# A graph attention layer on one core: the first stage in another order, and the first loads cut in halves

## What is computed

```python
h = jnp.maximum(_layernorm(x, axis=-1), 0.0)
# inside the layer, with node_features = h
h = node_features @ W.T + b_W
a1, a2 = (a_vec[:D_OUT], a_vec[D_OUT:])
e = (h @ a1)[:, None] + (h @ a2)[None, :] + b_a[0]
e = jnp.where(e > 0, e, 0.2 * e)
scores = jnp.where(adjacency_matrix > 0, e, jnp.float32(NEG_INF))
attention = jax.nn.softmax(scores, axis=1)
h_prime = attention @ h
# and outside it
x = x + h_prime
```

## Time and profile before

| | us |
|---|---|
| median of 3 runs | 201.71 (201.53 to 201.79) |
| profiled execution, its own time | 202.36 |
| span of the profiled execution | 200.8 |
| TensorE busy | 194.9 (97%) |
| VectorE busy | 183.0 (91%) |
| ScalarE busy | 147.9 (74%) |
| GpSimd busy | 52.4 (26%) |
| transfers | 75.66 MB, 377 GB/s over the span |

### The profile page before, as it was taken

One profiled execution on the slowest core, in us unless ns is written; L12 is line 12 of the kernel. 1 busy time (PEld: TensorE's weight loads), 2 busy tenths in 40 slices (PEclk: granted clock), 3 DMA queues, 4 the chain that ended last, 5 costly groups with the idle time before them and its releaser, 6 DMA issues.

```text
span 200.8 us, 7230 instructions
## 1 busy us (share of the span) xinstructions
PE 194.9 (97%) x3183; PEld 189.2 (94%) x3183; DVE 183.0 (91%) x265; ACT 147.9 (74%) x192; POOL 52.4 (26%) x66
## 2 busy tenths in 40 slices
PE   7969999999999999999999999999999999999993
PEld 7648889999999999999999999999999999999993
DVE  4779999999998799897999999999999999999745
ACT  2679879898882777689988888899588888996000
POOL 1002479699995010205000000072000000510000
PEclk9999999999999999999999999999999999999999
DMA  5999999999999999999999999999999999997012
GB/s 181 376 417 418 407 403 423 421 418 415 422 432 408 418 423 419 416 421 418 415 419 423 419 418 421 421 411 421 419 418 418 415 421 416 418 383 226 6 43 66
DMA packets 15968, 75.66 MB, mean 377 GB/s; under 512 B 1600, under 2 KB 5952, under 8 KB 7616
## 3 DMA queue, kind: packets, MB, share of 16 engines
q1 hardware_dynamic: 15792, 75.06, 91.7%
q10 hardware_dynamic: 144, 0.13, 0.3%
HBM read 73.08 MB, written 2.11 MB: 374 GB/s over the span
## 4 chain that ended last, share of the span: by engine, by line
PE 91%; DMA 4%; SPq 1%; DVE 1%; issue 1%; POOL 0%
PE ps L836 29%; PE ps L834 29%; PE ps L840 29%; DMA adj_sb<-in_adj_t 4%; PE ps L808 2%; PE ps L798 2%; SPq L268 1%; SPq L273 1%; PE ps L876 1%; DVE mask L476 0%; POOL bad L788 0%; DVE rden L504 0%; DVE rg L510 0%; DVE bad L519 0%; DVE upper L576 0%
## 5 line engine op out<-in xcount | busy, mean ns | idle before, releaser
L834 PE MATMUL ps<-V,w 128*128 128x129 f16 x1024 | 174.3, 221 | 0.0
L836 PE MATMUL ps<-V,w 128*128 128x129 f16 x1024 | 174.3, 221 | 0.0
L840 PE MATMUL ps<-V,w 128*128 128x129 f16 x1024 | 174.3, 221 | 0.0
L379 ACT ACTIVATE mask<-adj_sb 128x1024 bf16<-128x1024 int32 x126 | 125.5, 1056 | 28.6 <-DMA adj_sb<-in_adj_t 28.6
L459 DVE SCALAR_TENSOR_TENSOR w<-g_row,pairs,mask 128x1024 f32<-128x1024 f32 x96 | 120.5, 1320 | 5.5 <-ACT mask L379 3.6
L834 PEld LDWEIGHTS ps<-V,w 128*128 128x128 f16 x1024 | 100.2, 98 | 1.5 <-ACT H L340 0.7
L836 PEld LDWEIGHTS ps<-V,w 128*128 128x128 f16 x1024 | 100.2, 98 | 1.0 <-issue 1.0
L840 PEld LDWEIGHTS ps<-V,w 128*128 128x128 f16 x1024 | 100.2, 98 | 0.0
L459 DVE SCALAR_TENSOR_TENSOR w<-ps,pairs,mask 128x1024 f32<-128x1024 f32 x31 | 37.4, 1267 | 0.0
L785 POOL TENSOR_TENSOR xT<-xT,x_sb 128x512 f32<-128x512 f32 x6 | 11.5, 1932 | 79.8 <-ACT xT L394 79.8
L739 POOL TENSOR_TENSOR x_sb<-x_sb,b_row 128x512 f32<-128x512 f32 x8 | 10.0, 1301 | 0.0
(11 more groups left out here) (93 smaller groups left out, 63.8 us busy)
## 6 DMA issues: line engine op xcount, KB each, us to landing
adj_sb<-in_adj_t SPq DMA_DIRECT2D x64, 1024.0 KB, 10.3
xT<-in_x_t SPq DMA_DIRECT2D x8, 256.0 KB, 7.5
x_sb<-in_x_p SPq DMA_DIRECT2D x3, 512.0 KB, 10.9
g_row<-g_dram SPq DMA_DIRECT2D x1, 1536.0 KB, 10.3
out<-xT SPq DMA_DIRECT2D x3, 512.0 KB, 9.9
x_sb<-in_x_p SPq DMA_DIRECT2D x2, 256.0 KB, 4.2
out<-xT SPq DMA_DIRECT2D x1, 192.0 KB, 3.4
out<-xT SPq DMA_DIRECT2D x3, 64.0 KB, 1.6
```

The costliest lines, as they stand in the source:

```text
L379: nc.scalar.activation(mask[:, m % MASKS, r], adj_sb[:, m % HELD, r], ACT.Relu, scale=CONNECTED).then_inc(mask_ready, 1)
L834: nc.tensor.matmul(sums[:, bank, a, :], w16[:, m % SLOTS, col:col + P, 1], V[:, jt, 0, 0:NF], start=(jt == 0 and a == 0), stop=False, skip ...
L836: nc.tensor.matmul(sums[:, bank, a, :], w16[:, m % SLOTS, col:col + P, 1], V[:, jt, 1, 0:NF], start=False, stop=False, skip_group_check=True)
L840: last = nc.tensor.matmul(sums[:, bank, a, :], w16[:, m % SLOTS, col:col + P, 0], V[:, jt, 0, 0:NF], start=False, stop=(jt == NT - 1), ski ...
```

## The change

The first stage is put in another order on each engine, and two loads are cut in two.

- Loads: chunk 0 of xT comes in two halves of 128 KB, one by SP's queue and one by ScalarE's, and the packed weights stand behind the latter. Piece 0 of the adjacency comes in two halves of 512 KB: side 0 ahead of chunk 3 of xT and of x set 2, side 1 behind them. `early_mask` waits for side 0 alone, by a semaphore of its own.
- TensorE: `centre_chunk(0)` stands ahead of the matmuls on the weights; the column norms stand between the two h chunks, the constant behind them.
- ScalarE: relu of chunk 0 stands ahead of the two on the weights; the copy of H chunk 0 ahead of the roots.
- VectorE: statistics 0 and 1 in a row, then the norm; the constant `cc` behind the maximum of the scores; `gg` and what hangs on it behind `early_mask`; statistics 2 in one behind `weigh(0, 1)`; the reciprocal at the end of scores(0), now `ones_of(0)`, behind `scale_weights(0)`.

```diff
-                load_xt(0)
+                half = CT * P // 2
+                sp.dma_start(xT[:, 0:half], x_t[0, :, 0:half]).then_inc(xt_loaded[0], 16)
                 load_xt(1)
                 load_x(0)
                 load_x(1)
                 load_xt(2)
+                sp.dma_start(adj_sb[:, 0, 0:GC], adj_t[0, :, 0:GC]).then_inc(tile_loaded, 16)
+                load_xt(3)
                 load_x(2)
-                load_xt(3)
-                load_adj(0)
+                sp.dma_start(adj_sb[:, 0, GC:2 * GC], adj_t[0, :, GC:2 * GC]).then_inc(adj_loaded[0], 16)
...
+                half = CT * P // 2
+                act.dma_start(xT[:, half:2 * half], x_t[0, :, half:2 * half]).then_inc(xt_loaded[0], 16)
                 act.dma_start(wp[:], w_pack).then_inc(wp_loaded, 16)
...
+                relu_chunk(0)
                 act.wait_ge(wa_done, 1)
...
-                relu_chunk(0)
                 relu_chunk(1)
+                take_chunk(0)
                 roots_part()
-                take_chunk(0)
                 take_chunk(1)
...
                 def early_mask():
-                    dve.wait_ge(adj_loaded[0], 16)
+                    dve.wait_ge(tile_loaded, 16)
...
                 statistics(0)
+                statistics(1)
                 dve.wait_ge(norm_summed, 1)
-                nc.vector.tensor_reduce(norm[:], ps[:, 4, 0:DOUT], AX_X, ALU.max).then_inc(norm_ready, 1)
-                statistics(1)
+                nc.vector.tensor_reduce(norm[:], ps[:, G_BANK + 1, 0:DOUT], AX_X, ALU.max).then_inc(norm_ready, 1)
...
-                statistics(2, 0, 3)
-                scores(0)
...
-                statistics(2, 3, 5)
...
                 early_mask()
+                dve.wait_ge(root_ready, 1)
+                step_(nc.vector.tensor_scalar(gg[:, 0:1], root[:], 1e-30, None, ALU.max))
+                nc.vector.reciprocal(gg[:, 1:2], gg[:, 0:1]).then_inc(g_ready, 1)
+                dve.wait_ge(g_ready, 1)
+                step_(nc.vector.tensor_scalar(rstd[:, 2, 0:GI], rstd[:, 1, 0:GI], gg[:, 1:2], None, ALU.mult))
                 pack(0)
                 scale_weights(0)
+                ones_of(0)
                 products(0)
...
                 weigh(0, 1)
-                statistics(2, 5, 8)
+                statistics(2)
                 weigh(1, 0)
...
-                    pe.wait_ge(xt_loaded[c], 16)
+                    pe.wait_ge(xt_loaded[c], 32 if c == 0 else 16)
```

More of the change, by code:

```diff
@@ L170, in gat_layer_kernel @@
         x_loaded = [sem(f"x_loaded{i}") for i in range(len(SETS))]
+        tile_loaded = sem("tile_loaded")
         wp_loaded = sem("wp_loaded")
@@ L565, in scores, with ones_of @@
                                             ALU.mult).then_inc(scores_ready, 1)
+                    if part > 0:
+                        ones_of(part)
+                def ones_of(part):
+                    r = slice(*PARTS[part])
                     nc.vector.reciprocal(H[:, r, ONE], rstd[:, 2, r]).then_inc(ones_ready, 1)
@@ L616, in _ @@
                 statistics(0)
+                statistics(1)
                 dve.wait_ge(norm_summed, 1)
-                nc.vector.tensor_reduce(norm[:], ps[:, 4, 0:DOUT], AX_X, ALU.max).then_inc(norm_ready, 1)
-                statistics(1)
[L622 to L626, removed]
+                nc.vector.tensor_reduce(norm[:], ps[:, G_BANK + 1, 0:DOUT], AX_X, ALU.max).then_inc(norm_ready, 1)
                 dve.wait_ge(std_ready, 1)
                 nc.vector.reciprocal(rstd[:, 1, 0:GI], rstd[:, 0, 0:GI]).then_inc(std_ready, 1)
[L630 to L633, removed]
                 dve.wait_ge(std_ready, 2)
-                step_(nc.vector.tensor_scalar(rstd[:, 2, 0:GI], rstd[:, 1, 0:GI], gg[:, 1:2], None, ALU.mult))
-                statistics(2, 0, 3)
                 scores(0)
@@ L640, in _ @@
                 nc.vector.tensor_reduce(tt[:, 0:1], st[:, 0:GI, T], AX_X, ALU.max).then_inc(t_limits, 1)
-                statistics(2, 3, 5)
+                dve.wait_ge(cc_done, 1)
+                dve.wait_ge(wp_loaded, 16)
+                step_(nc.vector.tensor_scalar(cc[:, 1:2], ps[:, G_BANK, 0:1], wp[:, BA:BA + 1], None, ALU.add))
+                step_(nc.vector.tensor_tensor(cc[:, 0:1], cc[:, 1:2], ps[:, G_BANK, 1:2], ALU.add))
+                nc.vector.tensor_scalar(cc[:, 1:2], cc[:, 0:1], -SLOPE_OUT, SHIFT, ALU.mult, ALU.add).then_inc(cc_ready, 1)
                 dve.wait_ge(t_spread, 1)
@@ L850, in _ @@
                     nc.tensor.matmul(ps[:, 7, 0:P], ones[:], ones[:], start=True, stop=True)
+                pe.wait_ge(centre_ready, 1)
+                centre_chunk(0)
                 pe.wait_ge(wp_loaded, 16)
                 nc.tensor.matmul(ps[:, 5, 0:2], wp[:, 0:DIN], wp[:, AV:AV + 2], start=True, stop=True).then_inc(wa_done, 1)
-                nc.tensor.matmul(ps[:, 6, 0:2], wp[:, BW:BW + 1].to_broadcast([P, P]), wp[:, AV:AV + 2], start=True,
-                                 stop=True).then_inc(cc_done, 1)
[L856 to L861, removed]
+                centre_chunk(1)
+                pe.wait_ge(wa_ready, 1)
+                h_chunk(0)
+                pe.wait_ge(squares_ready, 1)
+                nc.tensor.matmul(ps[:, G_BANK + 1, 0:DOUT], ones[:], wsq[:], start=True, stop=True).then_inc(norm_summed, 1)
+                h_chunk(1)
+                nc.tensor.matmul(ps[:, G_BANK, 0:2], wp[:, BW:BW + 1].to_broadcast([P, P]), wp[:, AV:AV + 2], start=True,
+                                 stop=True).then_inc(cc_done, 1)
+                centre_chunk(2)
                 pe.wait_ge(norm_ready, 1)
-                h_chunk(1)
-                centre_chunk(2)
                 pe.wait_ge(t_limits, 1)
@@ L872, in _ @@
                 pe.wait_ge(t_bounds, 1)
+                pe.wait_ge(cc_ready, 1)
                 pe.wait_ge(pairs_ready, 1)
```

## The result

The change made the kernel slower: 203.19 us (median of 8 runs, 202.87 to 203.76) against 202.12 us for the kernel before, whose runs went on beside it (8 runs, 201.53 to 202.95). The ratio is 1.0047, with a 95% interval of 1.0026 to 1.0067. The forecast was 201.5, no difference that can be told. The profiled execution took 203.59 us, its span is 202.0, 1.2 us over the profiled one of before.

A forecast was written before the change was run, and what follows sets the result against it. TensorE, busy 97%, bounds the kernel: start of piece 0 plus all it must issue. Piece 0 0.5 us earlier, less a wait at piece 7, keeps 0.2: 202.36 to 202.2 profiled, median 201.5; range 201.1 to 202.1.

The forecast's parts named there:

- Step 1: Load queues: first half lands at 9.6 us, second about 12.7, later pieces keep their places; the extra transfer costs nothing.
- Rival D: Transfers: two more cost the train 1.3 us, relu chunk 6 ends 1.3 later; 0.8 us lost, 202.5; chance 0.05.
- slack of 0.54 us ahead of chunk 6: ScalarE ends relu of chunk 6 at 28.28 us, TensorE needs it at 28.86; set by the transfers.
- rival B: TensorE's level rises before 4.65 us, piece 0 starts 0.9 earlier, relu chunk 6 limits: gain 0.54, 201.2; chance 0.27.
- the forecast's own 0.2: Net gain in us that TensorE keeps of piece 0's 0.5 earlier start, after waiting for piece 7's weights.
- Step 2: TensorE's first centring starts near 4.65 us, its level rises near 5.4: 0.3 us gained, not 0.6.
- the gain of the head: First stage: piece 0 starts 0.5 us earlier on TensorE, `weigh(0, 1)` 0.55 earlier on VectorE, at 16.3.
- steps 5 to 8: VectorE: mask at 11.47 instead of 12.74, `pack` 0.60 earlier, piece 0 0.5 earlier, statistics of set 2 end 0.42 later.
- C: Rival: first stage gains nothing, statistics delay GpSimd's loop by 0.97 us, piece 7 starts 0.39 late, 202.1; chance 0.20.

The follow-up runs named there:

- e14: The changed kernel with the halves of adjacency piece 0 contiguous in DRAM, timed beside e13 on one chip: 202.52 us, ratio 1.0008 to the kernel before.
- e5: The kernel before, unchanged, run again for a second profile; no time given, ScalarE's mask of piece 3 starts at 25.77 us.
- e13: The changed kernel, unchanged, timed again beside e14 on one chip: 203.05 us, ratio 1.0033 to the kernel before.
- e9: The kernel before, orders untouched, with piece 0's contiguous first half between x set 2 and x chunk 3: 202.33 us against 202.51, ratio 0.9993.
- e2: The kernel before with the change's new orders but without its loads: 203.19 us, ratio 1.0045.
- e4: The changed kernel with adjacency piece 0 whole in its old place, x chunk 0 still in halves: 203.24 us, ratio 1.0034.
- e6: The changed kernel with piece 0 laid out half by half in DRAM, as e14 but on another chip: 202.88 us, ratio 1.0013.
- mended change: The changed kernel with contiguous halves, x set 2 ahead of the first half, four statistics of set 2 ahead of scores(0): ratios 0.9982 and 0.9988.
- e10: e2 with the statistics of set 2 cut as before (three, two, three): 202.98 us, ratio 1.0015 to the kernel before.
- e15: e11 with all eight statistics of set 2 behind `weigh(0, 1)` again: 202.57 us, ratio 1.0004 to the kernel before.
- e3: The changed kernel with x chunk 0 whole on SP's queue again, adjacency piece 0 still in halves: 203.49 us, ratio 1.0057.
- e11: The mended change, first timing: 202.18 us against 202.51 for the kernel before, ratio 0.9982.
- e17: e11 unchanged, timed again beside e18 on one chip: 202.08 us, ratio 0.9988 to the kernel before.
- e18: e15 unchanged, timed again beside e17 on one chip: 202.65 us, ratio 1.0015 to the kernel before.
- e12: The changed kernel, unchanged, run again for a second profile; no time given, ScalarE's mask of piece 3 starts at 26.59 us.
- e7: The kernel before with piece 0 in interleaved halves in its old place, `early_mask` waiting for the first: 203.12 us, ratio 1.0043.
- e16: e7 with the halves contiguous in DRAM: 202.49 us, ratio 1.0003 to the kernel before.

## Why the prediction was wrong

By its own steps:

1. **Step 1, the train of transfers, is the step that failed.** "The pieces behind keep their bytes and their places" was true and not enough: the bytes came at half the rate for two microseconds. The first half landed at 10.2 and not 9.6, the second at 13.4 and not 12.7, piece 3 at 26.98 and not 25.2. Costed at nothing, the layout cost 0.5 us beside e14, and put the limit at piece 3, behind which nothing that the rest gained could show. The extra issues came early enough, as forecast: e14 has them too and loses nothing that can be told.
2. Rival D had the right place and path, a slow train that reaches TensorE by piece 3 and relu of chunk 6, and a price (1.3 us, 202.5) near the 1.1 to 1.7 us by which the mask of piece 3 was later in the three profiles of the change. It had a chance of 0.05, "no byte is added", and its cause was wrong: it was not the number of transfers. Contiguous halves of 512 KB ran at 387 to 408 GB/s in e14, so the rule of the Trainium skill that was put beside D (DMA: Bandwidth & Descriptors, Bandwidth: batch to 1 MiB or more) did not bear on this train, which is never empty. The fixed cost of 2 us that went with it stands on that page of the Trainium skill for transfers issued by GpSimd (Anatomy of one DMA — SWDGE (gpsimd) path); these were issued by SP. Another entry of the Trainium skill stands nearer (DMA: Bandwidth & Descriptors, Latency and other measured facts): HBM rows at a large power-of-two pitch read slowly, and the cure is to pad the pitch or to lay the tiles out contiguously. It gives pitches of 512 KB and more, and calls its mechanism an inference; here the pitch is 8 KB. No run here shows the mechanism, but contiguous halves took the loss away in both pairs.
3. The slack of 0.54 us ahead of chunk 6 was one execution's. In e5 it was nothing. This made rival B, a gain of 0.54, too large from the start, and the forecast's own 0.2 unsafe: e13 had B's early piece 0 and was slower than before, and e9 had it and no gain that can be told.
4. Step 2 misread the level of TensorE's clock. 1.11 against 1.02 us was taken for a rise within the pair; but the second centring of the changed kernel and the third (9.77) take 1.10 at full rate too, behind a short matmul. The rise of before was earlier: both matmuls on `wp` took 0.36 us there, the first of them from 4.79. In e5 they took 0.51 and 0.37, so in e5 it came between them, near 5.2. In the change it came at about 6.5, 6.5 and before 4.5 in the three profiles (first centring 1.90, 1.90 and 1.02 us). In the first two the mask therefore started at 11.96 and 11.95, not at 11.47, and `weigh(0, 1)` at 16.82 in the first, not at 16.3: the gain of the head was gone.
5. The sizes in steps 5 to 8 held. Mask to `pack` 1.25 us (1.28 forecast), `pack` to products 0.95 (0.89), eight statistics 1.63 (1.64), and `weigh(7, 0)` moved by what the statistics moved: 19.64 less 18.72 is 0.92, and it ended at 41.51 + 1.27 = 42.78, 0.92 later than the earlier trace rows, where the forecast had 0.42 because it counted on 0.55 us of head start. With TensorE itself 1.2 us late, it waited for nothing.
6. C's condition, a `weigh(0, 1)` less than 0.4 us earlier, was met, and its path and price are in the traces of e2, e4, e6 and e14 (0.4 to 0.5 us at piece 7). But it is not what made any profile of the change slow.

The size of the loss, 1.07 us by the medians first shown and 0.70 in e13, is for the most part the layout (0.53, e13 less e14). What e14 keeps, 0.17 us over before with an interval that takes in nothing, agrees with its profile: h of chunk 7 is 0.35 us earlier than before, and the loop costs 0.4 to 0.5.

No version is shown to beat the kernel before. The mended change leans that way twice, by 0.18% and 0.12%, and both intervals reach just over 1.

## What to carry to other kernels

When a load is cut so that one part comes earlier, look at what a part is in DRAM: the half of each row is another access pattern than the half of the block, and here it took the time of the whole. Read the limit behind the one that is removed from more than one execution: a slack of half a microsecond in one profile was none in the next, and a gain of 1.1 us at the start of the products ended there. And a step that moves because its data comes later takes its consumers along, on every engine: price the loop, not the instruction. To see which of several late things sets the time, look for the intervals that stay the same from profile to profile, here 7.61, 16.49 and 167.4 us: they tell for each execution which chain held it.

## What the runs showed of the hardware

- **A first half of interleaved rows is slow, the second is not.** In the changed kernel the second half, the other 4 KB of each 8 KB, landed at 13.4 (4.74 + 8.7) behind x set 2 at 12.1 (4.24 + 7.9): 1.3 us for 512 KB, full rate (159 ns for a packet of 4 KB, against 262 in the first half), with the same row length and pitch. So the pitch alone is no cause, and the time of the first half was that of the whole block, as if its neighbours were fetched along. What does that stays open.
- **The rise of TensorE's level falls at very different times in executions of one program.** After the same warm-up, the first centring took 1.02 us in e10, e13 and e15, 1.20 to 1.52 in e3, e11, e14, e17 and e18, and 1.90 or 1.91 in the change, e12, e2, e4 and e6. In e7 and e16 it took 2.05 and the second still 1.91 and 1.92: the lower level held at least until the issue of the second centring was over, at 9.56 and 9.77 us, and piece 0 started at 18.30 and 18.56, 1.4 to 1.7 us later than in the earlier trace rows's execution. The granted clock column showed 1.0 all the while, in the stretches from 6 to 10 us of e7 too; only equal instructions side by side show the level.

```profile
5.58 2.05 PE L800 MATMUL ps<-xT,centre 128*128 128x512 f32 x2
7.43 0.64 PE L861 MATMUL ps<-wsq,ones 128*128 128x128 f32 x2
7.85 1.91 PE L800 MATMUL ps<-xT,centre 128*128 128x512 f32 x2
```

These are e7's, at the places where the earlier trace rows has 1.11, 0.38 and 1.02 us.

- **The executions of the change lie closer together.** e13's 12 runs span 202.95 to 203.45, e14's 201.91 to 203.22. A kernel that waits for piece 3 in any case does not show where TensorE's level rose. That is a reading of two spreads, not a test, and the first 8 runs of the change span 0.9 us (202.87 to 203.76).

Not tried: piece 3 ahead of the x loads that it now follows, which by all of this would be the first thing to move.
